# A 32-batch attention and channel-mix kernel: where the parts of the row maxima are transposed, and how far ahead operands are loaded

## The reference

```python
xn = _layernorm(x, axis=-1)
q = einsum('bsd,hde->bhse', xn, wq) + bq        # k and v alike
scores = softmax(einsum('bhst over e', q, k) * scale, axis=-1)
att = (scores @ v heads side by side) @ wo.T + bo
r = sigmoid(xr @ W_r.T); k_act = square(relu(xk @ W_k.T))   # xr, xk: xn mixed with the token before
out = x + att + r * (k_act @ W_v.T)
```

## Time and profile before

| | us |
|---|---|
| median of 3 runs (467.05 to 470.95) | 467.87 |
| the profiled execution | 468.32 |
| its span, first to last instruction | 466.2 |
| mean granted TensorE clock | 0.971 of full |

### The profile page before, as it was taken

The page is one execution under the profiler, slowest core; times in us unless marked ns, Lnnn a source line. Parts: engine busy times, 40 slices in busy tenths (PEclk is TensorE's granted clock), DMA queues, the critical chain, the costliest instruction groups (busy, mean ns, idle before and its releaser), DMA issues.

```text
span 466.2 us, 15769 instructions
## 1 busy us (share of the span) xinstructions
PE 449.2 (96%) x5254; PEld 275.1 (59%) x5254; DVE 400.7 (86%) x824; ACT 394.1 (85%) x896; POOL 366.5 (79%) x674
## 2 busy tenths in 40 slices
PE   6689999999999999999999999999999999999996
PEld 5245666666656666556665666566656666666554
DVE  7578999999988999899999999899998999989831
ACT  2138899999988999989998999989998999989894
POOL 6667888888888988888888888888888888887321
PEclk9558999999999999999999999999999999999999
DMA  4533465545345545344554544355545444455100
GB/s 135 158 116 99 124 162 148 142 134 150 109 140 148 157 127 155 108 132 130 148 159 129 156 139 127 104 147 155 159 137 138 136 126 125 137 151 147 51 15 24
DMA packets 86061, 60.43 MB, mean 130 GB/s; under 512 B 6224, under 2 KB 73808, under 8 KB 86032
## 3 DMA queue, kind: packets, MB, share of 16 engines
q1 hardware_dynamic: 86032, 60.06, 45.0%
HBM read 29.89 MB, written 29.36 MB: 127 GB/s over the span
## 4 chain that ended last, share of the span: by engine, by line
PE 88%; DMA 3%; issue 2%; DVE 2%; ACT 2%; SPq 1%; ACTq 0%; DVEq 0%; POOL 0%
PE bank_val L631 26%; PE bank_exp L707 18%; PE bank_max L717 11%; PE misc L736 5%; PE misc L758 4%; PE misc L646 4%; PE misc L665 3%; PE misc L747 3%; PE misc L799 3%; PE misc L792 3%; PE misc L673 2%; PE misc L773 2%; PE misc L768 1%; DMA ops<-spill 1%; DVE neg_max L557 1%
## 5 line engine op out<-in xcount | busy, mean ns | idle before, releaser
L557 DVE TENSOR_REDUCE neg_max<-bank_max 128x2 f32<-128x512 f32 x512 | 327.9, 684 | 37.9 <-PE bank_max L717 32.8
L454 ACT ACTIVATE probs<-bank_exp 128x512 f32<-128x512 f32 x504 | 273.5, 597 | 27.4 <-PE bank_exp L707 25.3
L717 PE MATMUL bank_max<-ops 48*128 48x256 bf16 x1024 | 161.5, 278 | 0.0
L707 PE MATMUL bank_exp<-ops 51*128 51x256 bf16 x1008 | 156.0, 273 | 4.2 <-issue 2.1
L631 PE MATMUL bank_val<-probs,val 128*25 128x256 f32 x2048 | 136.8, 385 | 0.8 <-ACT probs L454 0.8
L707 PEld LDWEIGHTS bank_exp<-ops 51*128 51x128 bf16 x1008 | 74.7, 95 | 66.2 <-issue 51.5
L631 PEld LDWEIGHTS bank_val<-probs,val 128*25 128x25 f32 x2048 | 50.5, 103 | 52.2 <-issue 27.0
L717 PEld LDWEIGHTS bank_max<-ops 48*128 48x128 bf16 x1024 | 77.0, 96 | 5.7
L356 POOL TENSOR_SCALAR xn<-x_in,moments,rstd 128x128 f32<-128x128 f32 x62 | 49.3, 802 | 0.0
L395 POOL TENSOR_TENSOR mixed_x<-mixed_x,xn_t 128x512 f32<-128x512 f32 x32 | 40.7, 1273 | 2.5
L370 POOL TENSOR_TENSOR qk_l<-qk_rest,qk_m 128x512 bf16<-128x512 f32 x31 | 36.0, 1163 | 2.5
(11 more groups left out here) (77 smaller groups left out, 627.9 us busy)
## 6 DMA issues: line engine op xcount, KB each, us to landing
ops<-spill SPq DMA_DIRECT2D x126, 192.0 KB, 3.4
spill<-qk_h SPq DMA_DIRECT2D x64, 192.0 KB, 3.3
spill<-qk_m SPq DMA_DIRECT2D x64, 128.0 KB, 1.9
x_in<-x SPq DMA_DIRECT2D x32, 128.0 KB, 2.2
spill<-qk_l SPq DMA_DIRECT2D x32, 128.0 KB, 1.8
y_out<-y SPq DMA_DIRECT2D x32, 128.0 KB, 1.9
ops<-shift SPq DMA_DIRECT2D x128, 6.0 KB
w<-weights SPq DMA_DIRECT2D x1, 448.0 KB, 3.0
```

What stands on the lines that cost most here:

```text
L454: nc.scalar.activation(probs[g % 2][:, u % G, :, :], exp_bank(u, live)[:, :, :], ACT.Exp, scale=SCALE).then_inc(exp_done[u], 1)
L557: nc.vector.tensor_reduce(out=neg_max[hf][:, :, r, pr], in_=bank_max[MAX_BANK[v]][:, :, :], axis=AX_X, op=ALU.max, negate=True).then_inc(m ...
L707: exp_mm = nc.tensor.matmul(exp_bank(u, live)[:, i, :], ops[p][rows, hf, 1, pr, i * P:(i + 1) * P], ops[p][rows, hf, 0, pr, :], start=True ...
L717: max_mm = nc.tensor.matmul(bank_max[MAX_BANK[v]][:, i, :], of[rows, max_hf, 0, max_pr, i * P:(i + 1) * P], of[rows, max_hf, 1, max_pr, :] ...
```

## The change

The transposes leave PE and ACT. `max_parts` becomes a tile of 128 x 2 x 128 bf16, of which 24 columns in each 128 hold parts and the others are cleared once by DVE. SP issues one transposing DMA for each half (`dma_start_transpose`, 64 KB) from `max_parts` to `shift`, which has the same shape, and the two shift loads wait for its landing, by `shift_done`, which now counts in sixteens. The identity in bf16, the PSUM route and the semaphore `shift_psum` are gone. POOL waits for the landing of the transpose before it writes the parts of the next batch.

There are four `ops` tiles in place of two. Both halves of batch t+2 are loaded in turn t, half 1 at the end of SP's turn, where before half 1 was loaded at the start of the turn after. Rows of ones for the two new tiles are copied from `ops[0]` by four small DMAs in the lead-in. SP's turn is in a new order, the store of y is of batch t-2, and POOL splits half 0 ahead of the sum `rest`.

The diff, cut to its core:

```diff
-        ops = [sb(f"ops{i}", [P, 2, 2, PR, S], BF16) for i in range(2)]
+        ops = [sb(f"ops{i}", [P, 2, 2, PR, S], BF16) for i in range(TURN)]
...
-        max_parts = [sb(f"max_parts{i}", [P, ST, 2, 3, PR], BF16) for i in range(2)]
-        shift = [sb(f"shift{i}", [2 * 3 * PR, S], BF16) for i in range(2)]
+
+        max_parts = [sb(f"max_parts{i}", [P, ST, P], BF16) for i in range(2)]
+        shift = [sb(f"shift{i}", [P, ST, P], BF16) for i in range(2)]
...
+            def load_ops(half, c, spilled, before):
...
-                    src = spill[p].rearrange("a s (e g pr) c -> g (s e) a (pr c)", e=E, pr=PR)[2 * half + r]
-                    sp.dma_start(ops[p][RG * r:RG * r + KS, half], src).then_inc(ops_in[half], 16)
...
+                    src = spill[c % 2].rearrange("a s (e g pr) c -> g (s e) a (pr c)", e=E, pr=PR)[2 * half + r]
+                    sp.dma_start(ops[c][RG * r:RG * r + KS, half], src).then_inc(ops_in[half], 16)
+
+            def copy_ones():
+
+                sp.wait_ge(k_filled[0], 1)
+                for i in range(2, TURN):
+                    for r in range(2):
+                        rows = slice(RG * r + KS, RG * r + KE)
+                        sp.dma_start(ops[i][rows, :, 1], ops[0][rows, :, 1]).then_inc(ones_in, 16)
...
-            def load_shift(half, p, count, before):
-
-                after(sp, shift_done[half], count)
...
+            def transpose_shift(half, count, before):
+                sp.wait_ge(parts_zero, 1)
+                sp.wait_ge(max_split[half], count)
+                after(sp, shift_in[half], before)
+                sp.dma_start_transpose(shift[half][:, :, :], max_parts[half][:, :, :].rearrange("p n c -> p (n c)")).then_inc(
+                    shift_done[half], 16)
+
+            def load_shift(half, c, done, before):
+
+                sp.wait_ge(shift_done[half], done)
                 after(sp, shift_in[half], before)
                 for r in range(2):
-                    sp.dma_start(ops[p][RG * r + KS:RG * r + KE, half, 0],
-                                 shift[half][3 * PR * r:3 * PR * (r + 1), :]).then_inc(shift_in[half], 16)
+                    sp.dma_start(ops[c][RG * r + KS:RG * r + KE, half, 0],
+                                 shift[half][3 * PR * r:3 * PR * (r + 1), :, :]).then_inc(shift_in[half], 16)
...
+            def store_y(b, parity, count):
+                sp.wait_ge(y_done, count)
+                sp.dma_start(out_dram[b], y[parity][:, :].rearrange("p (n d) -> p n d", n=ST)).then_inc(
+                    out_done[parity], 16)
+
             def step(t, c, n, moved, paired, quad, live):
                 p = c % 2
-                if live(4) and live(0):
-
-                    sp.wait_ge(x_bo_done, n(0))
-                    sp.wait_ge(xn_done, n(0))
-                    load_x(t + 4, c)
-                if live(1):
-
-                    after(sp, exp_scores[H - 1], n(-1))
-                    load_ops(1, 1 - p, moved(1, SPILLS), moved(0, 2))
+                if live(0):
+                    transpose_shift(1, n(0), moved(-1, 2))
                 if live(2):
                     after(sp, ops_in[0], moved(0, 2))
@@ -289,27 +299,38 @@
                     after(sp, spill_done, moved(1, SPILLS))
                     spill_part(p, "h", qk_h, h_done, n)
                 if live(0):
-                    load_shift(1, p, n(0), moved(-1, 2))
+                    load_shift(1, c, moved(0, 1), moved(-1, 2))
+                if live(4) and live(0):
+
+                    sp.wait_ge(x_bo_done, n(0))
+                    sp.wait_ge(xn_done, n(0))
+                    load_x(t + 4, c)
                 if live(2):
                     spill_part(p, "m", qk_m, (m_done, m_done), n)
                     spill_l(p, n)
-
-                    after(sp, exp_scores[HALF - 1], n(0))
+                if live(-2):
+                    store_y(t - 2, p, n(-2))
+                if live(1):
+                    transpose_shift(0, n(1), moved(0, 2))
+                if live(2):
+
+                    after(sp, exp_scores[H - 1], n(-1))
                     if not live(0):
                         sp.wait_ge(k_filled[p], 1)
                     if live(1):
-                        load_ops(0, p, moved(2, SPILLS), moved(1, 2))
+                        load_ops(0, (c + 2) % TURN, moved(2, SPILLS), moved(1, 2))
                     else:
-                        load_first_ops(p, moved(2, SPILLS))
+                        load_first_ops((c + 2) % TURN, moved(2, SPILLS))
                 if live(1):
-                    load_shift(0, 1 - p, n(1), moved(0, 2))
-                if live(-1):
-
-                    sp.wait_ge(y_done, n(-1))
-                    sp.dma_start(out_dram[t - 1], y[1 - p][:, :].rearrange("p (n d) -> p n d", n=ST)).then_inc(
-                        out_done[1 - p], 16)
-
-            steps(sp, step, (2, SPILLS))
+                    load_shift(0, (c + 1) % TURN, moved(1, 1), moved(0, 2))
+                if live(2):
+                    load_ops(1, (c + 2) % TURN, moved(2, SPILLS), moved(1, 2))
+                if live(1) and not live(0):
+                    copy_ones()
+                if live(-1) and not live(0):
+                    store_y(t - 1, 1 - p, n(-1))
+
+            steps(sp, step, (1, 2, SPILLS))
...
-                part = [max_parts[half][:, :, :, j, :] for j in range(3)]
+                parts = max_parts[half][:, :, 0:2 * 3 * PR].rearrange("p n (r j k) -> p n r j k", r=2, j=3)
+                part = [parts[:, :, :, j, :] for j in range(3)]
                 last_unit = HALF * (half + 1) - 1
                 after(pool, max_done[last_unit], count)
-                after(pool, shift_psum[half], before)
+                after(pool, shift_done[half], before)
                 nc.gpsimd.tensor_tensor(part[0], m[:, :, :, :], zero, ALU.add).then_inc(max_h[half], 1)
...
+                if live(1):
+                    split_max(0, n(1), moved(0, 1))
                 if live(-1):
...
-                if live(1):
-                    split_max(0, n(1), n(0))
...
-                    split_max(1, n(1), n(0))
...
-            steps(pool, step, (SPILLS,))
+                    split_max(1, n(1), moved(0, 1))
...
-            def move_shift(half, bank, count, before):
-                act.wait_ge(shift_psum[half], count)
-                after(act, shift_in[half], before)
-                nc.scalar.copy(shift[half][:, :], shift_in_bank(bank)).then_inc(shift_done[half], 1)
...
-                    if u == 1 and live(0):
-                        move_shift(1, near, n(0), moved(-1, 2))
...
-                    if u == 9 and live(1):
-                        move_shift(0, far, n(1), moved(0, 2))
...
+            for i in range(2):
+                last = nc.vector.memset(max_parts[i][:, :, :], 0.0)
+            last.then_inc(parts_zero, 1)
...
-                nc.vector.tensor_copy(ident16[:, :], ident[:, :]).then_inc(consts_made, 1)
...
-            def transpose_shift(half, bank):
-                for st in range(ST):
-                    last = nc.tensor.transpose(shift_in_bank(bank)[:, st * P:(st + 1) * P],
-                                               max_parts[half][:, st].rearrange("p r j k -> p (r j k)"),
-                                               ident16[:, :])
-                last.then_inc(shift_psum[half], 1)
...
+                        if u == 0 and live(-2) and not live(-4):
+                            pe.wait_ge(ones_in, 16 * 2 * (TURN - 2))
...
-                            exp_mm = nc.tensor.matmul(exp_bank(u, live)[:, i, :], ops[p][rows, hf, 1, pr, i * P:(i + 1) * P],
-                                                      ops[p][rows, hf, 0, pr, :], start=True, stop=True)
+                            exp_mm = nc.tensor.matmul(exp_bank(u, live)[:, i, :], ops[c][rows, hf, 1, pr, i * P:(i + 1) * P],
+                                                      ops[c][rows, hf, 0, pr, :], start=True, stop=True)
...
-                            rows, of = slice(RG * (1 - r), RG * (1 - r) + KS), ops[(p + ahead) % 2]
+                            rows, of = slice(RG * (1 - r), RG * (1 - r) + KS), ops[(c + ahead) % TURN]
...
-                    if u == 1 and live(0):
-                        pe.wait_ge(max_split[1], n(0))
+                    if u == 3 and live(0):
                         pe.wait_ge(act_r_done, n(0))
                         after(pe, qk_rest_done[1], n(2))
-                        transpose_shift(1, near)
-                    if u == 3 and live(0):
-                        pe.wait_ge(shift_done[1], n(0))
...
-                    if u == 9 and live(1):
-                        pe.wait_ge(max_split[0], n(1))
+                    if u == 11 and live(1) and live(0):
                         after(pe, att_t_done, n(-1))
                         after(pe, qk_rest_done[0], n(2))
-                        if not live(0):
-                            pe.wait_ge(consts_made, 2)
```

(3 more changed lines are left out.)

23 lines of the change are left out of this document (9 added, 14 removed).

## The result

| | before | after |
|---|---|---|
| median of the runs timed together (us) | 469.41 (467.05 to 472.17) | 485.27 (484.02 to 488.29) |
| the profiled execution | 468.32 | 484.02 |
| its span | 466.2 | 481.8 |

The ratio is 1.0345, 95% interval 1.026 to 1.043: slower. Where times of two kernels are compared, runs over 1.5% above the fastest of the same kernel are left out; this concerns one kernel alone, the long change further down. The time lies in the range given, but the likeliest case, no change, did not happen; the second rival's did, at the time worked out for it (484.7).

The account below looks back on a forecast made before the run. PE's sequence was taken to bound the kernel. From 468.3 us, 28 turns of 13.25 for 13.26 gave -0.3, eight halves outside them -0.7 and the lead-in +1.2: 468.5 us, range 461.5 to 492.

Parts of the forecast that it names:

- the likeliest case: Whole kernel: PE's gain and the loads' lateness cancel within 1%, 463.3 to 472.5 us; chance 0.38.
- the second rival: SP's queue: the transposing DMA holds it 1.25 us, landing after 3.4; loads 1.46 late, 484.7 us; chance 0.27.
- The bound and the gain: PE's sequence sets the turn; removing its transposes saves 0.19 us a turn, 13.26 to 13.07.
- SP's price: Two transposing DMAs a turn on SP: each holds the queue 0.71 us and lands 2.8 us after issue.
- T: How long a transposing DMA holds SP's queue: taken as 0.71 us, bounds 0.36 and 1.25.
- L: Time of a transposing DMA from issue to landing: taken as 2.8 us, bounds 1.8 and 3.9.
- the first rival: Stall-free turns: transpose holds SP's queue 0.4 us, lands after 2.2; loads 0.3 early, 463.0 us; chance 0.20.
- The wait at unit 14: PE at unit 14: loads of half 0 come 0.36 us late, shared to a 0.18 stall; turn 13.25.
- they land after 3.4 + 0.42 = 3.8 us: Loads of half 0 on SP: issued at 242.1, landed at 245.9, 0.36 us late for unit 14.
- POOL: POOL splitting half 0 ahead of rest: later work delayed about 0.25 us, covered by a 0.6 us wait; nothing.
- The third rival: Shift loads of half 1 late for PE's unit 8: 0.5 us stall a turn, some 481 us; chance 0.10.
- The lead-in: Kernel's start: transpose puts loads 0.56 us later, clearing tiles 0.3, four DMAs of ones; 1.2 us added.

Follow-up runs that it names:

- the long change: The change with its loop run twice instead of six times, 16 more turns written out: median 496.05 us; the first two runs, alone compared, 492.0, ratio 1.052.
- the copy kernel: The change with a plain DMA in place of the transposing one, same tiles, place, bytes and waits: 466.36 us, ratio 0.996.
- as the load of x shows: The change with the load of x and the store of y moved behind the loads of half 1: 755.96 us, ratio 1.62.

## Why the prediction was right and wrong
**The bound and the gain: right.** PE's sequence sets the turn. The transposes left it and took 0.2 us a turn with them, seen at full size in the copy kernel (0.21 for 0.19).

**SP's price: right in the sum, wrong in its parts.** T taken 0.71, measured 1.21; L taken 2.8, measured 2.3. Both errors cancel in the time at which the loads of half 0 go out: 8.02 us behind unit 0 (251.93 against 243.91) for a forecast of 7.96. Choosing the kind "short rows from SBUF" for T went wrong, since half the bytes took 1.13 and a plain DMA of the same bytes 0.54: here it is the kind of instruction that costs, not its bytes. The load of x and the store of y, at 0.80 each an estimate with nothing from the trace for the register instruction, took 0.74 and 0.69 with the gaps around them. The copy kernel, with T + L at 2.44, is what the first rival described (2.6); at 466.4 us it is 3 above that rival's 463.0: up to 167 us it had lost 3.1 against the kernel before, for which that rival's sum held 0.5.

The Trainium skill, VectorE: DVE Perf Modes, section The three transpose paths, had given 1309 ns for a 128x128 transpose by the DMA. The trace has 1.13 us for the issue and 2.2 from issue to landing, neither of them 1.31, and it does not bear out what I scaled from it: twice the size is 1.21 and 2.3, not 2.6. The Trainium skill, Advanced Engine Details and Errata, section X-Bar Transpose (TRN2), calls such DMAs as fast as ordinary ones. By landing that nearly holds here (2.3 against 1.9), by the time in SP's queue it doesn't (1.21 against 0.54), and the measurement decides.

**The wait at unit 14: right place, half the size.** Forecast 0.36 us late, shared to 0.18 a turn. Measured 0.81 in the turn followed above, and 6.1 us in nine of 18 turns, 0.34 a turn. The step that failed is "they land after 3.4 + 0.42 = 3.8 us": from the first issue to PE's start it is 4.26 (251.93 to 256.19), because the second issue starts 0.57 later, its landing takes 3.6 and not the median 3.4, and PE starts 0.09 behind it. That is 0.46 more; the loads went 0.06 later than forecast and unit 14 itself is due 0.07 later, so the lateness is 0.36 + 0.46 + 0.06 - 0.07 = 0.81. Halving it was right, but as an alternation, not as equal stalls: a turn in which unit 14 waited lets the next transpose go out 0.95 us ahead of unit 0 (229.84 against 230.79), the turn after it only 0.19 (243.72 against 243.91), which is where the forecast had put it. The same rule had put the landing before the change at 244.7, 1.0 us ahead of unit 14; the trace has 244.9 (3.0 to 3.7 us from issue to landing in that pair), 0.8 ahead. The loop's turn comes out at 13.63 - 13.39 = +0.24 where 0.34 - 0.19 = +0.15 follows from these numbers, and -0.01 was forecast. The 0.09 left are small waits of PE and a busy time that fell by 0.13 and not 0.19; what makes them is open.

**POOL, the shift loads of half 1, four tiles: right at nothing.** Order and tiles alone were 467.57, as before. The third rival did not happen: unit 8 waits in no turn, since L was 2.3.

**The lead-in: too small.** Forecast 1.2, measured 2.6. SP's first transpose and the loads of half 0 behind it:

```profile
23.55 1.29 SPq L261 DMA_TRANSPOSE shift<-max_parts  x1
24.97 2.25 SPq L239 DMA_DIRECT2D ops<-spill  x2
```

The loads start 1.28 us later than in the earlier trace rows (24.97 against 23.69) for 0.56 in the forecast: 1.29 for T and not 0.71. And their own issue takes 2.25 where it took 1.09, a long issue once more. PE's first score matmuls on these loads (the max scores of batch 1, which start where unit 14 stands in other turns) start at 30.41 against 27.85, and with that the 2.6 are there. The four copies of ones took 3.00 us of SP's queue, not 4 x 0.42 = 1.68; they stand behind these loads, and with them in the kernel that has order and tiles alone no loss shows.

**What no step of the forecast held:** the price of code that is run for the first time. 6.0 us are lost up to 173 and 2.7 at the end, over half of the loss; at the 0.24 a turn of the repeated loop the nine turns up to 173 would have lost 2.2, so some 3.8 of their 6.0 go with new code, and how much of the 2.7 does is not shown. The slack of 1.0 us in the earlier trace rows was treated as idle; it was what absorbed the long issues, which the kernel before has in about every second turn of new code. The trace of before showed it, in its own long issues (1.69 and 1.77 us for a pair, above), where the median of an ops load is 0.42, and the maximum, 1246 ns, stood in the row from which I took it as a mere upper bound for T. The second rival's 484.7 is met for another sum than its own: it had 15.1 us in the loop and 2 in the lead-in, while the runs show 4.3 in 18 turns of the loop, 2.6 in the lead-in and 8.7 in the other turns. By mechanism it is right (the transpose holds the queue, loads of half 0 are late for unit 14), by size it was luck.

## What to carry to other kernels
A slack between a load's landing and its reader has to be set against the worst issue, not the median: look at the turns in which code is run for the first time, and at the maximum in the row of issues, before you spend the slack. An engine's instruction that costs 0.1 us inside a saturated sequence may be cheaper than a transfer whose issue alone is ten times that, if the queue it goes to feeds the same engine. And before moving an issue to a place where nobody waits, look up its reader, as the load of x shows.

## What the runs showed of the hardware
A transposing DMA within SBUF, 128x256 of bf16, holds SP's queue for 1.21 us and lands after 2.3; at 128x128 it is 1.13 and 2.2, and a plain DMA of the first size 0.54 and 1.9. Behind 384 KB of loads it lands after 3.5 in the median and up to 5.1. Single issues of SP are up to 1.7 us longer (2.63 for a pair of 0.96) where code is run for the first time, between 45 and 150 us about one a turn in the change and one in two turns in the kernel before, and between 150 and 395 us, where the loop repeats, none. The clock is no part of what is lost there: the granted clock is full (1.00, that is 2.4 GHz) between 45 and 395 us in both kernels. In the lead-in, from 28 to 45 us, it is 0.65 after and 0.73 before.
